# Quantised feed-forward: rows times their steps before the first product, and the last group of the feed-forward on VectorE alone

## The chip, the cores and the metric

The kernel runs on one core of a Trainium2 chip. Its engines are TensorE (PE; its weight loads are PEld), VectorE (DVE), ScalarE (ACT) and GpSimd (POOL); SyncE (SP) issues most transfers. Each engine works through its own instructions in order and waits for semaphores that the others raise. The metric is the device time of one execution in microseconds (us); lower is better.

## The reference, cut to what matters

The program is a cross-attention layer with a top-32 selection, a state-space convolution, a GELU feed-forward (phase "ff"), and a quantised feed-forward with a depthwise convolution (phase "bf"). The change touches the end of ff and all of bf. With T = 4096 rows, D = 512 and 2048 hidden features, bf computes:

```python
def act_quant(x):
    scale = 127.0 / jnp.clip(jnp.max(jnp.abs(x), axis=-1, keepdims=True), 1e-05)
    return jnp.clip(jnp.round(x * scale), -128, 127) / scale
def weight_quant(w):
    scale = 1.0 / jnp.clip(jnp.mean(jnp.abs(w)), 1e-05)
    return jnp.clip(jnp.round(w * scale), -1, 1) / scale
...
xq = x + jax.lax.stop_gradient(act_quant(x) - x)
wq = w + jax.lax.stop_gradient(weight_quant(w) - w)
...
h = bit_linear(x, w1)                               # rows quantised, weights -1, 0, 1
h = depthwise_conv1d(h.transpose(0, 2, 1), conv_w, conv_b)   # three taps along the rows
h = h.transpose(0, 2, 1)
h = jax.nn.silu(h)
return bit_linear(h, w2)                            # h quantised again by its row's maximum
...
x = x + _L0_xattn_ref(_layernorm(x, axis=-1), ...)
x = x + _L0_ffn_ref(_layernorm(x, axis=-1), ...)
```

So a row of the input of bf is a row of small integers (`q`, exact in bf16) times one number, its step.

## The kernel before, in words

**ff** (`feed_forward`) takes the 4096 rows in 8 groups (QUADS) of 4 tiles of 128 rows. The work that closes a group (add the second product, layer norm, add x, layer norm again, find each row's step, round, turn the integers on TensorE and store them) is laid between the products of the next group. Only the last group (`last_g`) has nothing beside it: its closing work stands after the last matmul. `out_moments`, `normalise_out`, `x_moments`, `normalise_x`, `find_steps`, `round_x` and `quantise_x` run on VectorE, each over all four tiles; between `normalise_out` and `x_moments` GpSimd (`back`) multiplies each tile by `g_norm_out` and adds it to `x`. TensorE turns the four tiles of `q` one after the other through one PSUM bank (`turn_q`), ScalarE copies each out (`copy_q`) and then stores all four at once into `scratch_qT`, at column 512 g + 1. Then all engines meet (`end_phase`), and bf begins.

**bf** (`bit_feed_forward`) takes the rows in 9 blocks of 456 (448 in the last). Step i = 8 n + j of 72 handles block n and the pair j of 8 pairs of 128 hidden features. In a step

- TensorE (`first`) makes 8 bf16 matmuls of 458 columns, integer weights times integer rows, into `hp[i % 2]`; it may do so once the taps of step i - 2 have read that bank;
- VectorE (`dequantise`) multiplies both halves in PSUM by `rowstep`, the steps of the rows spread over all partitions;
- ScalarE (`first_tap`) writes the first tap into `conv`, VectorE (`add_taps`) adds the other two with four instructions, ScalarE takes `silu`, then `measure` writes the absolute values into `size`, and VectorE (`raise_high`) keeps the maximum over the features in `high`.

After the eighth pair VectorE folds `high` to `top`, TensorE turns it (`turn_top`, step 8 n + 10), VectorE finds the rows' steps (`steps`, step 8 n + 11, after its taps), TensorE spreads them (`spread_steps`, step 8 n + 12) and ScalarE copies them (`copy_scale`, end of step 8 n + 12). That releases GpSimd for the block: 8 multiplications (`scaling`) and 3 roundings (`quantise`). ScalarE rounds the other five pairs (`round_up`, `round_down`) in steps 8 n + 14 to 8 n + 18. From step 8 n + 19 TensorE makes the second product (`second`: 8 bf16 matmuls of 512 columns in a step), and VectorE (`finish`) adds it to `x2`, four times in a block. The last block has its last five pairs scaled and rounded on VectorE (`quantise_last`).

SP loads the integers and steps of a block two ahead into double buffers, and loads and stores `x2` a block at a time. The order is written out by hand: the loops over i of each engine fix it.

Of the kernel before, what the change touches and what calls it, by code (L numbers as in the profile page):

```python
# [1818 lines left out]
def feed_forward(nc, sem, const, a, mean, dram):  # L1819
# [7 lines left out]
    with scope:  # L1827
# [43 lines left out]
            "xt_free", "qT_stored", "rowstep_stored", "x_stored", "biased", "edges", "passed")}  # L1871
# [5 lines left out]
        with nc.Block() as block:  # L1877
# [111 lines left out]
            def _(pool):  # L1989
# [48 lines left out]
            def _(dve):  # L2038
# [188 lines left out]
                round_x(last_g)  # L2227
                quantise_x(last_g)

            @block.scalar  # L2230
            def _(act):
# [4 lines left out]
                act.dma_start(dram["qT"][:, :, 0], zero[:], allow_slow_non_contiguous=True).then_inc(s["qT_stored"], 16)  # L2236
                act.dma_start(dram["qT"][:, :, T + 1], zero[:], allow_slow_non_contiguous=True).then_inc(s["qT_stored"], 16)
# [15 lines left out]
                def copy_q(g, k):  # L2253
# [3 lines left out]
                    nc.scalar.activation(qT[:, :, k * P:(k + 1) * P], fl[1][:].bitcast(BF16)[:, 0:D].rearrange("p (c t) -> p c t", t=P),  # L2257
# [62 lines left out]
                act.wait_ge(s["qT_stored"], 16 * (QUADS + 2))  # L2320
# [3 lines left out]
            def _(pe):  # L2324
# [116 lines left out]
def bit_feed_forward(nc, sem, const, a, mean, dram, out):  # L2441
# [9 lines left out]
    BY_ACT, LAST_BY_ACT = 5, 3  # L2451
    STEPS_AT, SCALE_AT, ROUND_AT, SECOND_AT = JC + 3, JC + 4, JC + 6, 2 * JC + 3
    with scope:
        W1q = sb("bf_W1q", [P, DC, HID], BF16)
        W2q = sb("bf_W2q", [P, FC, D], BF16)
        rowstep = sb("bf_rowstep", [P, 2, STEP + 2])
# [3 lines left out]
        qin = sb("bf_qin", [P, 2, DC, STEP + 2], BF16)  # L2460
        x2 = sb("bf_x2", [P, 2, QUAD, D])
# [33 lines left out]
        with nc.Block() as block:  # L2495
            @block.sync
            def _(sp):
                def load(n):

                    if n >= 2:  # L2500
                        sp.wait_ge(s["first_done"], JC * (n - 1))
                    sp.dma_start(qin[:, n % 2, :, 0:QUAD * rows(n) + 2],
                                 dram["qT"][:, :, STEP * n:STEP * n + QUAD * rows(n) + 2]).then_inc(s[f"q_in{n % 2}"], 16)

                def load_steps(n):

                    if n >= 2:
# [428 lines left out]
```

## Time and profile before

| | |
|---|---|
| median of 3 runs | 4088.72 us (4087.74 to 4088.88) |
| the profiled execution | 4093.82 us, its span 4092.0 us |
| end of the last ff matmul | 3557.3 us of the span |
| first and last bf matmul start | 3608.5 and about 4085.8 us |
| busy over the span | PE 77%, DVE 74%, ACT 55%, POOL 38% |

How to read it: times are microseconds from the start of the span; a row of a timeline has start, duration, engine, line, operation, out<-in, shapes, count, and in brackets how long the engine sat idle before and what released it. A row of windows has the stretch, its length, busy time and instruction count of each engine, the granted TensorE clock as a share of full speed (1.00 is 2.4 GHz, 0.50 is 1.2 GHz), the DMA share and the rate. bf16 and f32 are the types that the rows name; TensorE's operands that are declared as F32R are written f32 too.

### The profile page before, as it was taken

The numbers are of one execution on the slowest core, as the hardware profiler recorded it, in microseconds if no ns is written. First come the engines' busy times: TensorE is split into PE (matmuls) and PEld (weight loads), VectorE is DVE, ScalarE is ACT, GpSimd is POOL, SyncE is SP. The second block draws the span as 40 slices with busy tenths as digits, with TensorE's granted clock in tenths as the row PEclk, the third lists the DMA queues.
The fourth block names the chain that finished last, engine by engine and source line by source line (L and its number), as shares of the span: only waits on it lengthen the run. The fifth ranks groups of instructions, "written<-read, shape, count | busy, mean of one in ns | idle before, by whom it ended". The sixth has DMA issues, their size and how long they took to land. (4 is left out here: it accounts for less than half of the span.)

```text
span 4092.0 us, 53285 instructions
## 1 busy us (share of the span) xinstructions
PE 3136.8 (77%) x16624; PEld 1983.5 (48%) x16624; DVE 3013.2 (74%) x7501; ACT 2241.5 (55%) x2905; POOL 1561.5 (38%) x1275
## 2 busy tenths in 40 slices
PE   7545857878786688777978777599999999746776
PEld 3222424444443344445755554377777777612333
DVE  7699999999999999975579986234444444469996
ACT  4575959898986898861133332133333333247774
POOL 0024636665564556656201000213333322206664
PEclk9756878888877787888989988799999999868887
DMA  8700000000000000003214334544344443331111
GB/s 320 267 7 8 10 7 12 10 10 12 9 10 9 10 9 10 9 6 106 81 38 97 90 88 98 152 124 128 118 127 127 129 127 103 95 86 36 54 44 55
DMA packets 264316, 290.46 MB, mean 71 GB/s; under 512 B 55452, under 2 KB 177438, under 8 KB 263012
## 3 DMA queue, kind: packets, MB, share of 16 engines
q1 hardware_dynamic: 240728, 254.05, 20.7%
q10 hardware_dynamic: 20268, 18.34, 1.6%
q0 software_dynamic: 3040, 14.94, 0.9%
q8 instruction: 102, 1.67, 0.2%
q14 instruction: 178, 1.46, 0.1%
HBM read 218.82 MB, written 68.45 MB: 70 GB/s over the span
## 5 line engine op out<-in xcount | busy, mean ns | idle before, releaser
L1094 PE MATMUL up<-ctx,attnT 128*128 128x384 f32 (+1 forms) x1664 | 713.7, 585 | 41.6 <-ACT attnT L966 41.6
L1066 PE MATMUL score<-KT,q 64*128 64x512 f32 (+1 forms) x1792 | 388.4, 527 | 377.5 <-ACT S L928 279.6
L823 DVE MAX8 cand<-S 128x8 f32<-128x146 f32 (+1 forms) x2816 | 601.2, 296 | 57.6 <-ACT S L928 38.6
L782 POOL TENSOR_TENSOR S<-S 128x512 f32<-128x512 f32 (+1 forms) x224 | 424.6, 1928 | 351.5 <-DVE S L828 351.5
L1094 PEld LDWEIGHTS up<-ctx,attnT 128*128 128x128 f32 (+1 forms) x1664 | 365.6, 230 | 314.4 <-issue 154.8
L828 DVE SCALAR_TENSOR_TENSOR S<-S,tops,E 128x3202 f32<-128x3202 f32 x128 | 472.8, 3757 | 14.6 <-ACT E L957 14.6
L1066 PEld LDWEIGHTS score<-KT,q 64*128 64x128 f32 x1792 | 175.5, 239 | 580.1 <-ACT S L928 435.2
L928 ACT ACTIVATE S<-score 128x1024 f32<-128x1024 f32 (+1 forms) x448 | 402.8, 931 | 89.4 <-PE score L1066 88.8
L2163 DVE TENSOR_TENSOR ff_gelu<-ff_whole,ff_gelu 128x512 fp32r<-128x512 f32 x128 | 99.4, 777 | 429.7 <-ACT ff_gelu L2290 429.7
L935 ACT ACTIVATE E<-S,below 128x3202 bf16<-128x3202 f32 x128 | 379.6, 2966 | 38.6 <-DVE below L865 17.7
L957 ACT ACTIVATE E<-S,ebias 128x3202 f32<-128x3202 f32 x128 | 376.2, 2964 | 22.5 <-DVE S L828 12.4
L2399 PE MATMUL ff_acc<-ff_W,ff_gelu 128*128 128x512 f32 x1024 | 345.5, 398 | 0.0
L2289 ACT ACTIVATE ff_whole<-ff_fp,ff_b 128x512 f32<-128x512 f32 x128 | 87.8, 686 | 397.0 <-PE ff_fp L2384 396.7
L2384 PE MATMUL ff_fp<-ff_hT,ff_W 128*128 128x512 f32 x1024 | 267.2, 404 | 4.7 <-ACT ff_gelu L2290 3.2
L2761 PE MATMUL bf_hp<-bf_qin,bf_W1q 128*128 128x458 bf16 (+1 forms) x576 | 160.8, 435 | 117.7 <-DVE bf_conv L2602 98.1
L789 POOL TENSOR_TENSOR S<-S 128x512 f32<-128x512 f32 (+1 forms) x217 | 243.5, 1159 | 8.4 <-issue 8.4
L2556 POOL TENSOR_TENSOR bf_silu<-bf_silu,bf_scale 128x912 f32<-128x912 f32 (+1 forms) x67 | 162.6, 2465 | 212.9 <-ACT bf_scale L2713 212.9
L2399 PEld LDWEIGHTS ff_acc<-ff_W,ff_gelu 128*128 128x128 f32 x1024 | 193.5, 189 | 45.4
L2384 PEld LDWEIGHTS ff_fp<-ff_hT,ff_W 128*128 128x128 f32 x1024 | 190.9, 191 | 48.2 <-ACT ff_gelu L2290 4.1
L793 POOL TENSOR_TENSOR S<-S 128x512 f32<-128x512 f32 (+1 forms) x217 | 207.6, 992 | 4.9 <-issue 4.9
L2602 DVE SCALAR_TENSOR_TENSOR bf_conv<-bf_hp,bf_taps,bf_conv 128x456 f32<-128x456 f32 (+1 forms) x288 | 185.8, 687 | 25.2 <-ACT bf_conv L2686 14.3
L2399 PE MATMUL ff_acc<-ff_w_low,ff_gelu 128*128 128x512 f32 x512 | 203.1, 397 | 0.0
(378 smaller groups left out, 5890.7 us busy)
## 6 DMA issues: line engine op xcount, KB each, us to landing
s_hankel<-scratch_K SPq DMA_DIRECT2D x128, 256.0 KB, 4.4
ff_w_low<-scratch_w1l SPq DMA_DIRECT2D x112, 256.0 KB, 2.6
ff_w_low<-scratch_w2l SPq DMA_DIRECT2D x112, 256.0 KB, 2.7
xt_prep<-in_x SPq DMA_DIRECT2D x8, 1024.0 KB, 8.3
scratch_xt<-xt_prep SPq DMA_DIRECT2D x8, 1024.0 KB, 8.2
next_prep<-in_ffn_w_t POOLq DMA_DIRECT2D x8, 1024.0 KB, 11.3
q<-scratch_qt SPq DMA_DIRECT2D x128, 64.0 KB, 1.9
mod_xt<-in_x_turned SPq DMA_DIRECT2D x32, 256.0 KB, 2.7
```

The source lines that it names most:

```text
L782: nc.gpsimd.tensor_tensor(S[:, b, 0, chunk(j)], S[:, b, 0, chunk(j)], S[:, b, 1, chunk(j)], ALU.add).then_inc(s["summed01"], 1)
L789: nc.gpsimd.tensor_tensor(S[:, b, 0, chunk(j)], S[:, b, 0, chunk(j)], S[:, b, 2, chunk(j)], ALU.add).then_inc(s["summed02"], 1)
L793: nc.gpsimd.tensor_tensor(S[:, b, 0, chunk(j)], S[:, b, 0, chunk(j)], S[:, b, 3, chunk(j)], ALU.add).then_inc(s["summed"], 1)
L823: nc.vector.max(cand[:, h, 8 * k:8 * k + 8], S[:, b, h, k * SEG:min((k + 1) * SEG, G)])
L828: nc.vector.scalar_tensor_tensor(S[:, b, h, :], S[:, b, h, :], tops[:, b, h, TOP - 1:TOP], E[:, h % 2, :], ALU.is_ge, ALU.mult).then_inc(s ...
L928: nc.scalar.activation(S[:, b, PAIRS_OF_HEADS[p], chunk(j)], score[bank(p, j)][:, :, 0:w], ACT.Copy).then_inc(s["score_copied"], 1)
L935: nc.scalar.activation(signs, S[:, b, h, :], ACT.Sign, bias=below[:, h:h + 1], accum_out=count[:, h:h + 1]).then_inc(s["counted"], 1)
L957: nc.scalar.activation(E[:, h % 2, :], S[:, b, h, :], ACT.Exp, bias=ebias[:, b, h:h + 1], scale=SCALE).then_inc(s["e_ready"], 1)
L1066: last = nc.tensor.matmul(score[bank(p, j)][:, e, 0:w], lhsT=q[at, b, part, h // 2, :], rhs=KT[at, h // 2, chunk(j)], start=(part == 0), s ...
L1094: last = nc.tensor.matmul(up[:, 0:DV], lhsT=attnT[0:w, e, c - 4 * g, :], rhs=ctx[0:w, c, :], start=(c == 0), stop=(c == GC - 1))
L2384: last = nc.tensor.matmul(fp[f % 2][:], lhsT=left, rhs=hT[:, h_part, c, :], start=(j == 0), stop=(j == len(terms) - 1))
L2399: last = nc.tensor.matmul(acc[:, k, :], lhsT=gelu[:, g_part, F % RING, k * P:(k + 1) * P], rhs=right, start=(f == 0 and j == 0), stop=(f = ...
```

## The change: what it does

1. **Last group of ff.** GpSimd only adds `b_norm_out` to x (`x_shifted`) and takes no further part. VectorE does the multiplication by `g_norm_out` and the addition too, in an order that rotates through the tiles: in one round it normalises tile i, multiplies tile i - 1, adds tile i - 2 and takes the moments of tile i - 3, with a drain after each round. Rounding and quantising go tile by tile, the turned tiles use two PSUM banks in turn, and `qT` is stored in two halves of 256 columns.
2. **`scratch_qT`** has a margin of 32 columns at either end, so that a group's store starts at a multiple of 64 bytes.
3. **First product of bf.** A row's integers are multiplied by its step before the product: GpSimd (`spread`, for block 0 VectorE) writes `rows_of_x`, 4 x 458 columns, in f32; ScalarE (`high_x`) rounds it to F32R, VectorE (`low`) takes the rest, and TensorE multiplies both parts by the weights, now F32R as well: 16 matmuls in a step, where there were 8. `dequantise` goes. The weights come in as bf16 (into the second half of `bf_silu`, free at that time) and are cast by VectorE (pieces 0 and 1) and GpSimd (2 and 3).
4. **Order on ScalarE:** `first_tap(i)` now precedes `silu(i-1)`; it waits for TensorE and no longer for VectorE. The absolute values go back into `conv`.
5. **SP** loads one block of integers and steps at a time (single buffers), and loads and stores `x2` tile by tile.

```diff
-                add_hidden(last_g)
-                out_moments(last_g)
-                normalise_out(last_g)
-                x_moments(last_g)
...
+                for i in range(QUAD + 3):
+                    if i < QUAD:
+                        v.tensor_scalar(at[i], at[i], mv["out"][:, i, 0:1], rstd["out"][:, i:i + 1], ALU.subtract, ALU.mult)
+                    if 1 <= i < QUAD + 1:
+                        v.tensor_tensor(at[i - 1], at[i - 1], rows["g_norm_out"][:], ALU.mult)
+                    if 2 <= i < QUAD + 2:
+                        v.tensor_tensor(x[:, i - 2], x[:, i - 2], at[i - 2], ALU.add).then_inc(s["x_ready"], 1)
+                    if 3 <= i:
+                        v.bn_stats(stats["x"][:, i - 3, :], x[:, i - 3])
+                    dve.drain()
...
-                        act.dma_start(dram["qT"][:, :, QUAD * P * g + 1:QUAD * P * (g + 1) + 1], qT[:]).then_inc(s["qT_stored"], 16)
+                        act.dma_start(dram["qT"][:, :, MARGIN + QUAD * P * g:MARGIN + QUAD * P * (g + 1)], qT[:]).then_inc(s["qT_stored"], 16)
...
+    HIGH_AT, LOW_AT = 3, 4
...
-        W1q = sb("bf_W1q", [P, DC, HID], BF16)
+        W1q = sb("bf_W1q", [P, DC, HID], F32R)
...
+                def spread(n):
+                    w = QUAD * rows(n) + 2
+                    pool.wait_ge(s["q_in"], 32 * (n + 1))
+                    pool.wait_ge(s["parts_ready"], n)
+                    nc.gpsimd.tensor_tensor(rows_of_x[:, :, 0:w], qin[:, :, 0:w], rowstep[:, 0:w].unsqueeze(1).broadcast_to([P, DC, w]),
+                                            ALU.mult).then_inc(s["dequantised"], 1)
...
                 for n in range(BLOCKS - 1):
+                    if n + 2 < BLOCKS:
+                        spread(n + 2)
                     pool.wait_ge(s["scale_ready"], n + 1)
...
-                    for e in range(2):
-                        at = hp[i % 2][:, e, 0:w]
-                        v.tensor_tensor(at, at, rowstep[:, n % 2, 0:w], ALU.mult).then_inc(s["dequantised"], 1)
+                    dve.wait_ge(s["high_ready"], n + 1)
+                    v.tensor_tensor(x_parts[:, n % 2, 1, :, 0:w], rows_of_x[:, :, 0:w], x_parts[:, n % 2, 0, :, 0:w].bitcast(F32),
+                                    ALU.subtract).then_inc(s["parts_ready"], 1)
...
+                def high_x(n):
+                    w = QUAD * rows(n) + 2
+                    act.wait_ge(s["dequantised"], n + 1)
+                    if n >= 2:
+                        act.wait_ge(s["first_done"], JC * (n - 1))
+                    nc.scalar.activation(x_parts[:, n % 2, 0, :, 0:w], rows_of_x[:, :, 0:w], ACT.Copy).then_inc(s["high_ready"], 1)
...
                 for i in range(ALL + ROUND_AT):
+                    if i % JC == HIGH_AT and i < ALL - JC:
+                        high_x(i // JC + 1)
...
+                    for x in range(2):
+                        if j == 0 and x == 1:
+                            pe.wait_ge(s["parts_ready"], n + 1)
+                        for e in range(2):
+                            f = 2 * j + e
+                            for c in range(DC):
+                                last = nc.tensor.matmul(hp[i % 2][:, e, 0:w], lhsT=W1q[:, c, f * P:(f + 1) * P], rhs=x_parts[:, n % 2, x, c, 0:w],
+                                                        start=(c == 0 and x == 0), stop=(c == DC - 1 and x == 1))
```

VectorE's order at the end of ff, before: each operation over the four tiles, with GpSimd's part between the second and third of these rows.

```order
L2102 TENSOR_SCALAR ff_xt<-ff_xt,ff_mv_out,ff_rstd_out 128x512 x4
L2108 BN_STATS ff_stats_x<-ff_x 128x6 x4
L2058 BN_AGGR ff_mv_x<-ff_stats_x 128x2 x4
L2063 RECIPROCAL ff_rstd_x<-ff_rstd_x 128x4
L2114 TENSOR_SCALAR ff_xt<-ff_x,ff_mv_x,ff_rstd_x 128x512 x4
```

And now, in the same place:

```order
L2240 TENSOR_SCALAR ff_xt<-ff_xt,ff_mv_out,ff_rstd_out 128x512 x2
L2242 TENSOR_TENSOR ff_xt<-ff_xt,ff_g_norm_out 128x512
L2240 TENSOR_SCALAR ff_xt<-ff_xt,ff_mv_out,ff_rstd_out 128x512
L2242 TENSOR_TENSOR ff_xt<-ff_xt,ff_g_norm_out 128x512
L2244 TENSOR_TENSOR ff_x<-ff_x,ff_xt 128x512
L2240 TENSOR_SCALAR ff_xt<-ff_xt,ff_mv_out,ff_rstd_out 128x512
L2242 TENSOR_TENSOR ff_xt<-ff_xt,ff_g_norm_out 128x512
L2244 TENSOR_TENSOR ff_x<-ff_x,ff_xt 128x512
L2246 BN_STATS ff_stats_x<-ff_x 128x6
```

GpSimd's multiplication and addition have moved between the normalisations, to VectorE.

GpSimd in bf, before, from its first block on (`bf_silu` is the block's values, `bf_gq` the rounded ones):

```order
L2556 TENSOR_TENSOR bf_silu<-bf_silu,bf_scale 128x912 x8
L2564 TENSOR_SCALAR bf_gq<-bf_silu 128x912 x3
L2556 TENSOR_TENSOR bf_silu<-bf_silu,bf_scale 128x912 x8
L2564 TENSOR_SCALAR bf_gq<-bf_silu 128x912 x3
L2556 TENSOR_TENSOR bf_silu<-bf_silu,bf_scale 128x912 x8
```

And now (`bf_rows` is `rows_of_x`):

```order
L2601 TENSOR_TENSOR bf_rows<-bf_qin,bf_rowstep 128x1832
L2620 CAST bf_W1q<-bf_silu 128x4x512 x2
L2601 TENSOR_TENSOR bf_rows<-bf_qin,bf_rowstep 128x1832
L2606 TENSOR_TENSOR bf_silu<-bf_silu,bf_scale 128x912 x8
L2614 TENSOR_SCALAR bf_gq<-bf_silu 128x912 x3
L2601 TENSOR_TENSOR bf_rows<-bf_qin,bf_rowstep 128x1832
L2606 TENSOR_TENSOR bf_silu<-bf_silu,bf_scale 128x912 x8
L2614 TENSOR_SCALAR bf_gq<-bf_silu 128x912 x3
```

One multiplication of 1832 columns stands behind the three roundings of each block.

ScalarE in bf, steps 8 n + 3 and 8 n + 4, before:

```order
L2698 ACTIVATE bf_silu<-bf_conv 128x912
L2686 ACTIVATE bf_conv<-bf_hp,bf_tap_bias,bf_taps 128x456 x2
L2706 ACTIVATE bf_size<-bf_silu 128x912
L2698 ACTIVATE bf_silu<-bf_conv 128x912
L2686 ACTIVATE bf_conv<-bf_hp,bf_tap_bias,bf_taps 128x456 x2
L2706 ACTIVATE bf_size<-bf_silu 128x912
L2713 ACTIVATE bf_scale<-bf_step_rows 128x456
```

And now:

```order
L2742 ACTIVATE bf_x_parts<-bf_rows 128x1832
L2753 ACTIVATE bf_conv<-bf_hp,bf_tap_bias,bf_taps 128x456 x2
L2765 ACTIVATE bf_silu<-bf_conv 128x912
L2771 ACTIVATE bf_conv<-bf_silu 128x912
L2753 ACTIVATE bf_conv<-bf_hp,bf_tap_bias,bf_taps 128x456 x2
L2765 ACTIVATE bf_silu<-bf_conv 128x912
L2771 ACTIVATE bf_conv<-bf_silu 128x912
L2778 ACTIVATE bf_scale<-bf_step_rows 128x456
```

The copy of the next block's rows (`high_x`) stands ahead of the first tap of step 8 n + 3; the first tap has moved ahead of the silu.

## Rows read from the trace of the kernel before

**Rows 1.** Windows: four blocks of bf by their first dequantise, and a stretch of ff.
```profile
3611.90:3652.40 40.50, 22.35 (x64) 7.51 (x62) 35.02 (x54) 24.03 (x31) 0.00 (x0) 0.63 0.38 142
3652.40:3697.10 44.70, 25.23 (x70) 8.91 (x70) 41.09 (x67) 28.79 (x37) 18.01 (x8) 0.66 0.06 16
3697.10:3744.20 47.10, 28.73 (x118) 13.78 (x118) 43.14 (x68) 34.67 (x43) 31.93 (x13) 0.92 0.06 16
...
3888.40:3936.50 48.10, 34.61 (x134) 17.13 (x134) 44.49 (x70) 34.89 (x43) 28.99 (x12) 0.85 0.16 54
...
3400.00:3550.00 150.00, 148.14 (x664) 118.16 (x663) 58.50 (x108) 47.74 (x73) 29.63 (x20) 1.00 0.38 108
```

**Rows 2.** Waits from 3500 us on: who waited for whom, total, times, longest.
```profile
PE bf_hp L2761 <- DVE bf_conv L2602: 98.1, 47, 4.5
```

**Rows 3.** Timeline of VectorE in the sixth block of bf.
```profile
3862.48 0.68 DVE L2625 TENSOR_REDUCE bf_most<-bf_mp 114x4 f32<-114x512 f32 x1
...
3864.86 1.18 DVE L2590 TENSOR_TENSOR bf_hp<-bf_hp,bf_rowstep 128x458 f32<-128x458 f32 x2
...
3877.41 1.11 DVE L2616 TENSOR_TENSOR bf_high<-bf_size,bf_high 128x912 f32<-128x912 f32 x1
3878.62 2.66 DVE L2602 SCALAR_TENSOR_TENSOR bf_conv<-bf_hp,bf_taps,bf_conv 128x456 f32<-128x456 f32 x4
3881.20 0.74 DVE L2644 SCALAR_TENSOR_TENSOR bf_x<-bf_op,bf_undo,bf_x 114x512 f32<-114x512 f32 x1
...
3883.12 2.51 DVE L2616 TENSOR_TENSOR bf_high<-bf_size,bf_high 128x912 f32<-128x912 f32 x1
```

**Rows 4.** Timeline of GpSimd: the eighth block's scaling and rounding.
```profile
4012.31 19.22 POOL L2556 TENSOR_TENSOR bf_silu<-bf_silu,bf_scale 128x912 f32<-128x912 f32 x8 [18.84 <-ACT bf_scale L2713]
4031.48 9.74 POOL L2564 TENSOR_SCALAR bf_gq<-bf_silu 128x912 bf16<-128x912 f32 x3
```

**Rows 5.** Timeline of ScalarE: a first tap, and the copy that releases Rows 4.
```profile
3889.29 1.34 ACT L2686 ACTIVATE bf_conv<-bf_hp,bf_tap_bias,bf_taps 128x456 f32<-128x456 f32 x2
...
4011.68 0.54 ACT L2713 ACTIVATE bf_scale<-bf_step_rows 128x456 f32<-128x456 f32 x1
```

**Rows 6.** Groups by form, ScalarE and GpSimd: count, then busy us, mean ns.
```profile
L541 ACT ACTIVATE junk_prep<-next_prep 128x2048 bf16<-128x2048 f32 x8 | 15.3, 1911 | 0.7
...
L2017 POOL TENSOR_TENSOR ff_x<-ff_x,ff_b_norm_out 128x2048 f32<-128x2048 f32 x8 | 36.9, 4615 | 58.3 <-DMA ff_x<-in_x 58.3
...
L2556 POOL TENSOR_TENSOR bf_silu<-bf_silu,bf_scale 128x896 f32<-128x896 f32 x3 | 8.3, 2785 | 6.6 <-ACT bf_scale L2713 6.6
```

**Rows 7.** Timeline of TensorE: F32R in ff, then bf's start and sixth block.
```profile
3527.96 2.03 PE L2384 MATMUL ff_fp<-ff_hT,ff_W 128*128 128x512 f32 x8
...
3608.54 6.01 PE L2761 MATMUL bf_hp<-bf_qin,bf_W1q 128*128 128x458 bf16 x16 [19.47 <-DMA bf_W1q<-scratch_w1q]
...
3865.00 1.03 PE L2779 MATMUL bf_step_rows<-bf_diag,bf_every 114*128 114x456 f32 x2 [1.45 <-DVE bf_diag L2635]
...
3881.42 1.72 PE L2761 MATMUL bf_hp<-bf_qin,bf_W1q 128*128 128x458 bf16 x8
3882.98 1.89 PE L2797 MATMUL bf_op<-bf_W2q,bf_gq 128*114 128x512 bf16 x8
```

**Rows 8.** Timeline of VectorE and ScalarE at the end of ff.
```profile
3563.46 3.81 DVE L2102 TENSOR_SCALAR ff_xt<-ff_xt,ff_mv_out,ff_rstd_out 128x512 f32<-128x512 f32 x4
...
3576.84 1.92 DVE L2114 TENSOR_SCALAR ff_xt<-ff_x,ff_mv_x,ff_rstd_x 128x512 f32<-128x512 f32 x4
...
3583.84 1.43 DVE L2140 TENSOR_SCALAR ff_q<-ff_xt 128x512 bf16<-128x512 f32 x4
...
3589.11 0.60 ACT L2257 ACTIVATE ff_qT<-ff_fl 128x512 bf16<-128x512 bf16 x1 [0.76 <-PE ff_fl L2367]
```

**Rows 9.** DMA issues from 3580 us to 3625 us: size, us to landing.
```profile
scratch_qT<-ff_qT ACTq DMA_DIRECT2D x1, 512.0 KB, 11.0
```

**Rows 10.** Windows: the last store.
```profile
4088.00:4090.00 2.00, 0.00 (x0) 0.00 (x0) 0.00 (x0) 0.00 (x0) 0.00 (x0) 0.65 1.00 310
```

More of the change, by code:

```diff
@@ L1812 @@
 LEAST = 1e-5
+MARGIN = 32
 LEVEL = 127.0
@@ new lines, in load_x, with store @@
+                def load_x(n, k):
+                    if n >= 1:
+                        sp.wait_ge(s[f"stored{k}"], 16 * n)
+                    sp.dma_start(x2[0:rows(n), k], dram["x2"][rows_at(n, k), :]).then_inc(s[f"x_in{k}"], 16)
+                def store(n, k):
+                    sp.wait_ge(s["y_ready"], QUAD * n + k + 1)
+                    sp.dma_start(out[rows_at(n, k), :], x2[0:rows(n), k]).then_inc(s[f"stored{k}"], 16)
+                load(0)
+                for k in range(HID // BANK):
+                    sp.dma_start(raw_w1[:, :, k * BANK:(k + 1) * BANK], dram["w1q"][:, :, k * BANK:(k + 1) * BANK]).then_inc(s[f"w1_in{k}"], 16)
+                    if k == 0:
+                        sp.dma_start(taps[:], a["conv_w_cols"]).then_inc(s["taps_in"], 16)
+                        sp.dma_start(tap_bias[:], a["conv_b_cols"]).then_inc(s["taps_in"], 16)
@@ L2545, in _ @@
-                for b in range(2):
-                    sp.wait_ge(s[f"stored{b}"], 16 * ((BLOCKS + 1 - b) // 2))
+                for k in range(QUAD):
+                    load_x(0, k)
+                for m in range(BLOCKS + 3):
+                    if m + 2 < BLOCKS:
+                        load(m + 2)
+                    if 0 <= m - 3 < BLOCKS:
+                        store(m - 3, 2)
+                    if 0 <= m - 3 < BLOCKS - 1:
+                        load_x(m - 2, 1)
+                    if 0 <= m - 3 < BLOCKS:
+                        store(m - 3, 3)
+                    if 0 <= m - 3 < BLOCKS - 1:
+                        load_x(m - 2, 2)
+                    if 0 <= m - 2 < BLOCKS:
+                        store(m - 2, 0)
+                    if 0 <= m - 3 < BLOCKS - 1:
+                        load_x(m - 2, 3)
+                    if 0 <= m - 2 < BLOCKS:
+                        store(m - 2, 1)
+                    if 0 <= m - 2 < BLOCKS - 1:
+                        load_x(m - 1, 0)
@@ L2548, in _ @@
+                for k in range(QUAD):
+                    sp.wait_ge(s[f"stored{k}"], 16 * BLOCKS)
             @block.gpsimd
@@ L2668, in _ @@
                         steps((i - STEPS_AT) // JC)
+                    if i % JC == LOW_AT and i < ALL - JC:
+                        low(i // JC + 1)
                     if i == ALL - JC + SCALE_AT:
@@ L2703, in measure @@
                     act.wait_ge(s["silu_done"], i + 1)
[L2704 to L2706 removed]
+                    nc.scalar.activation(conv[:, j % DEEP, :, 0:QUAD * rows(n)], part(n, j), ACT.Abs).then_inc(s["sized"], 1)
                 def copy_scale(n):
```

166 lines of the change are left out of this document (83 added, 83 removed).

## The prediction, made before the changed kernel was run

> **What bounds the kernel now.** I read the stretches first, then the waits, then the timelines of single engines. The change reaches the end of ff and all of bf, 535 us of 4092; the rest I leave as it is. In bf a block takes 40.5 us at the start and 48.1 us from the fourth on, and VectorE is busy for 44.5 of these 48.1, TensorE for 34.6 and GpSimd for 29.0 [rows 1]. TensorE waits for the taps on VectorE, 98.1 us in 47 waits [rows 2]. So VectorE sets the pace. One step costs it: dequantise 1.27 us (3864.86 to the next instruction, 1.18 busy and a drain), the maximum 1.21 (3877.41 to 3878.62), the four tap instructions 2.58 (3878.62 to 3881.20), together 5.06 [rows 3], and 8 x 5.06 = 40.5 is the first block exactly. The rest of a later block is the steps (2.38, 3862.48 to 3864.86), four finishes of 0.74, one fold, and stretched maxima such as the one of 2.51 us instead of 1.11 [rows 3].
>
> **The change in bf, part by part.**
> VectorE loses 16 dequantise instructions a block, 8 x 1.27 = 10.2 us, and gains one `low` of 1832 columns: two SBUF inputs in f32, by the maximum's 1.11 us for 912 columns at most 2.2, I take 2.1 [rows 3]. Its busy time in a block falls from 44.5 to about 36 us, and it is no longer the bound.
>
> TensorE's first product doubles to 16 matmuls of 458 columns, now F32R. The trace has F32R only at 512 columns: 8 in 2.03 us with the last one's 0.4, a pitch of 0.233 [rows 7]. The bf16 matmul of 458 columns has 1.56 / 8 = 0.195 (3881.42 to 3882.98) and that of 512 (1.89 - 0.38) / 7 = 0.216 [rows 7]. So F32R has 0.017 more at 512. If that is a constant, 458 columns take 0.21, which I use; the bounds are 0.195 (no surcharge) and 0.233 (the weight load sets the pitch, whatever the columns). A block costs TensorE 8 x (16 x 0.21 + 8 x 0.216) = 40.7, the spread of the steps 0.9, four small transposes 0.6 at most by the 458-column pitch: 42.1 us, with bounds of 40.1 and 45.
>
> The Trainium skill (TensorE: Matmul & The Clock Gate, Weight-path perf modes) says that the fast weight load works for 128 weights of any type but FP32. It speaks against the change, since the weights become F32R; by it the pitch would be nearer the upper bound, and that is the first rival below.
>
> GpSimd gains `spread`, 1832 columns with two inputs. By the 2048-column addition of 4.615 us (2.25 ns a column) it costs 4.1, by the scaling at 19.22 / 8 = 2.40 for 912 columns (2.63 ns) 4.8; at the rounding's 9.74 / 3 = 3.25 (3.6 ns) it would be 6.5 [rows 4, 6]. I take 4.7. It stands behind the block's roundings, and ScalarE's `high_x` of the next but one block waits for it ahead of the first tap of step 8 n + 3, in front of everything that leads to the next `copy_scale`. That closes a loop: scaling and rounding 28.9 [rows 4], spread 4.7, high_x 1.73 (the 2048-column activation takes 1.91, less 216 columns) [rows 6], first tap 1.34 [rows 5], taps 2.66 and steps 2.38 [rows 3], spread_steps 1.03 [rows 7], copy_scale 0.54 [rows 5]: 43.3 us. Seven handovers of 0.08 (ScalarE ends at 4012.22, GpSimd starts at 4012.31) [rows 4, 5] make it 43.9. Queued behind the waiting high_x are the taps, so VectorE, and two steps later TensorE, wait with it. The loop is 1.8 longer than TensorE's own 42.1 and is what I expect to be late next. ScalarE itself carries 34.9 [rows 1] + 1.7, about 37 of 43.9.
>
> Blocks, before and after: the first is 8 x 3.79 (maximum and taps) + 2.1 - 1.2 (no maximum for its first pair) plus some start-up, 33.0 against 40.5, -7.5. The second has steps, fold and low beside: 36.5 against 44.7, -8.2. The third gets the second product and the loop: 44.5 against 47.1, -2.6. Blocks four to eight: 5 x (43.9 - 48.1) = -21. The steps of the ninth up to `copy_scale` of the eighth: no high_x, -2. From there on (4012.2 to the end) the chain is as before: GpSimd scales and rounds 28.9, then second product, `quantise_last`, second product; 0.
>
> The start of bf is later. Before, the first matmul starts at 3608.5 when the weights are in, at half the clock: 16 matmuls in 6.01, 0.376 each [rows 7]. Now VectorE first multiplies (2.1), ScalarE copies (1.73) while VectorE casts the weights, with two handovers 4.0; then step 0 has 16 matmuls at half clock instead of 8, +3.0; the first dequantise before the tap goes, -0.7. Together +6.3. The rows' steps, whose load now gates the start, I take as landing with the weights. GpSimd's two casts are hidden: pairs 4 and 6 are wanted 16 and 24 us after the first.
>
> Sum in bf up to the last store: 6.3 - 7.5 - 8.2 - 2.6 - 21 - 2 = -35.0.
>
> **The end of ff.** From 3563.46 to 3576.84 the chain takes 13.4 us: normalisation at 3.81 for four, since GpSimd works beside it, where the next one takes 1.92 without [rows 8], then GpSimd's product and sum tile by tile. On VectorE alone it is 1.9 + 12 x 0.62 (512 of 912 columns at 1.11) [rows 3] + seven drains of 0.15 + the same 1.1 of aggregate and root = 11.5, -1.9; the drains of the rotated first part give back 0.6. Rounding tile by tile lets the first transpose start 1.2 earlier; the last copy, now at 3589.71 because each turn and copy through one bank takes 1.36, follows VectorE's pitch of 0.95: -1.3 [rows 8]. Together -3.8.
>
> The store of `qT` lands 11.0 us after its issue [rows 9], and no engine computes in that time. It goes to 2-byte aligned columns; now the last half of 256 KB starts on a 64-byte multiple. Bounds: 11 (alignment does nothing) and 3; I take 4.5, so -6.5.
>
> The last store: 896 KB at 310 GB/s take 2.9 us [rows 10]; now only the last quarter is left: -2.0.
>
> Sum: -35.0 - 3.8 - 6.5 - 2.0 = -47.3. Against the profiled execution's 4093.8 that is 4046.5; that execution is 5.1 us above the median of the runs, so the median should be 4041, and I say 4042.
>
> **Rivals.**
> A. TensorE is the bound: F32R at 458 columns keeps the pitch of 0.233. Block 45 us plus one handover, 45.3; against 43.9 that is 1.4 x 5 and about 3 in the earlier blocks: +10, 4052. For: 0.233 is measured, 0.21 is not. Against: nothing in the rows says that the pitch is the load's and not the columns'.
> B. GpSimd is slower than taken: the scaling takes 2.785 when VectorE uses SBUF all the time [rows 6] against 2.40 [rows 4], 8 x 0.38 = 3.1 a block, or `spread` takes 6.5. Loop 45.7 to 47, six blocks: +11 to +18, 4056. For: VectorE's maxima are stretched beside GpSimd now, 2.51 for 1.11 [rows 3]. Against: VectorE has fewer instructions than before. The Trainium skill (GPSIMD Engine Reference, Specifications) says that GpSimd shares its SBUF interfaces with VectorE and that they contend when VectorE has two SBUF inputs; `low` and the maxima are such. The trace agrees for the maxima, and by that rule this rival gains.
> C. The store of `qT` is no faster: +6.5, 4049.
> D. Slower than before: TensorE falls back to 1.2 GHz. Its mean clock in bf is 0.63 to 0.92 of full now [rows 1], and at half clock a step costs 16 x 0.376 + 8 x 0.42 (0.376 by the columns) = 9.4, a block 78. With 30% of the matmuls there a block is 42.1 + 0.3 x 36 = 53: (53 - 43.9) x 8 = +73, 4115. It turns the sign from a share of about 22% on. Against: in ff, where TensorE is busy for 148 of 150 us, the clock is 1.00 [rows 1], and here it would be busy for 42 of 44.
>
> The change certainly does what it says; the instructions are counted in the order.
>
> **Chances.** Forecast (4036 to 4048) 0.50, A 0.17, B 0.15, C 0.10, D 0.05, the rest (a faster GpSimd or a gain in the early blocks) 0.03. The range of 8 in 10 takes in the bounds of the pitch, the store and `spread`: 4029 to 4062. About 0.2% (8 us) is what a measurement of this kernel tells from no change: faster 0.94, same 0.02, slower 0.04.
>
> **What would show it.** A steady block of 43.9 us between first taps; ScalarE waiting for `bf_rows` at high_x once a block, about 1 to 2 us; TensorE's clock at 1.00 from the third block on; F32R pitch of 0.21 in `bf_hp`; GpSimd's new instruction at 4.7 us; first taps of bf some 6 us later after the weights; `qT` landing under 5 us. If TensorE has no wait left in a steady block, A holds; if high_x waits long and the block is over 45, B; a clock under 0.8 in steady blocks would make the whole forecast wrong.

## The result, and the profile after

The changed kernel takes 4064.73 us (4064.64 to 4065.74, 4 runs) against 4088.80 us before (4087.74 to 4089.04): a ratio of 0.9942, 95% interval 0.9925 to 0.9959. A second measurement gave 4063.50 us against 4090.17 (0.9934, 0.9918 to 0.9951). So it is faster, by 24 us and not by the 47 forecast; 4064.7 lies outside the range of 4029 to 4062.

The work ahead of the changed part ends at 3557.3 us in the trace of before and at 3553.3 after, though it is the same; in twelve more traces it ends between 3549.0 and 3557.9. So I count from marks: the end of the last ff matmul, the start of bf (GpSimd's first memset), GpSimd's first scaling of each block. The stretch from the start of bf to the first scaling is 71.5 to 73.9 us in the eleven other traces of the changed bf and its variants, so a difference of 2 us in that row says little.

| us | before | after | change | forecast |
|---|---|---|---|---|
| last ff matmul to start of bf | 44.8 | 39.9 | -4.9 | -10.3 |
| start of bf to 1st scaling | 77.0 | 71.9 | -5.1 | -5.3 |
| 1st to 2nd | 45.0 | 47.2 | +2.2 | -5.4 |
| 2nd to 8th | 288.2 | 270.7 | -17.5 | -24.3 |
| 8th to the end | 79.7 | 79.8 | +0.1 | -2.0 |
| sum | | | -25.2 | -47.3 |

The forecast's column is made of its own terms: +6.3 - 7.5 and half of -8.2 up to the first scaling (it comes at the end of step 12), the other half of -8.2 and of -2.6 to the second, and the rest behind.

Windows of the changed kernel, which answer to [rows 1] (stretch, length, busy time and count of PE, PEld, DVE, ACT, POOL, clock, DMA share, GB/s). First the first block by its taps, then the stretch from first to second scaling, then a steady block.

```profile
3610.09:3644.91 34.82, 27.91 (x127) 23.09 (x126) 29.38 (x39) 26.70 (x33) 9.41 (x4) 1.00 0.28 83
3665.16:3712.37 47.21, 37.31 (x152) 29.71 (x151) 41.63 (x50) 36.21 (x44) 36.11 (x12) 0.90 0.05 16
3848.49:3893.89 45.40, 42.76 (x199) 32.91 (x199) 40.87 (x55) 36.77 (x44) 35.51 (x12) 1.00 0.19 58
```

VectorE's 44.5 of 48.1 have become 40.9 of 45.4, TensorE's 34.6 have become 42.8 at a clock of 1.00. No engine is busy all the time. The waits from 3740 to 3990 us (who for whom, total, times, longest) show who holds whom:

```profile
ACT bf_conv L2753 <- PE bf_hp L2833: 30.9, 14, 4.4
...
PE bf_step_rows L2851 <- DVE bf_diag L2689: 8.2, 5, 2.0
...
ACT bf_x_parts L2742 <- POOL bf_rows L2601: 3.2, 4, 0.9
...
PE bf_hp L2833 <- DVE bf_conv L2654: 2.9, 5, 1.0
```

TensorE's 98.1 us of waiting for the taps [rows 2] have become 17.0 over the same part of the program, and 2.9 in this window. What is left is mainly a wait for the steps once a block, and ScalarE's wait for GpSimd's `rows_of_x`. GpSimd's timeline of one block, to set beside [rows 4]:

```profile
3848.49 21.42 POOL L2606 TENSOR_TENSOR bf_silu<-bf_silu,bf_scale 128x912 f32<-128x912 f32 x8 [9.90 <-ACT bf_scale L2778]
3869.88 10.56 POOL L2614 TENSOR_SCALAR bf_gq<-bf_silu 128x912 bf16<-128x912 f32 x3
3880.41 3.59 POOL L2601 TENSOR_TENSOR bf_rows<-bf_qin,bf_rowstep 128x1832 f32<-128x1832 bf16 x1
3893.89 21.34 POOL L2606 TENSOR_TENSOR bf_silu<-bf_silu,bf_scale 128x912 f32<-128x912 f32 x8 [9.89 <-ACT bf_scale L2778]
```

21.4 + 10.55 + 3.6 + 9.9 = 45.4: that is the whole block. ScalarE and TensorE between `spread` and the next scale, in the same block:

```profile
3884.03 1.73 ACT L2742 ACTIVATE bf_x_parts<-bf_rows 128x1832 fp32r<-128x1832 f32 x1 [0.94 <-POOL bf_rows L2601]
3885.67 1.34 ACT L2753 ACTIVATE bf_conv<-bf_hp,bf_tap_bias,bf_taps 128x456 f32<-128x456 f32 x2
...
3893.27 0.55 ACT L2778 ACTIVATE bf_scale<-bf_step_rows 128x456 f32<-128x456 f32 x1 [1.32 <-PE bf_step_rows L2851]
```

```profile
3863.61 3.58 PE L2833 MATMUL bf_hp<-bf_x_parts,bf_W1q 128*128 128x458 f32 x16
3867.03 1.89 PE L2869 MATMUL bf_op<-bf_W2q,bf_gq 128*114 128x512 bf16 x8
...
3892.20 1.03 PE L2851 MATMUL bf_step_rows<-bf_diag,bf_every 114*128 114x456 f32 x2 [2.04 <-DVE bf_diag L2689]
```

`high_x` starts as soon as GpSimd is done, and everything up to `bf_scale` follows it: so the loop of the prediction is closed. Sixteen F32R matmuls take 3867.03 - 3863.61 = 3.42 us, 0.214 each (forecast 0.21, against 0.376 at half clock in [rows 7]).

### The profile page after: what moved, and what is told of

Read it like the earlier page. It is cut to its first block and busy times, and to the rows that moved or that the text cites. A ratio compares the mean times of both kernels' runs of the same rounds, so it can differ in the third digit from the quotient of the medians.

```text
span 4062.9 us, 54357 instructions
## 1 busy us (share of the span) xinstructions
PE 3210.7 (79%) x17200; PEld 2131.9 (52%) x17200; DVE 2987.0 (74%) x7377; ACT 2258.4 (56%) x2914; POOL 1602.9 (39%) x1277
## 5 line engine op out<-in xcount | busy, mean ns | idle before, releaser
L1094 PE MATMUL up<-ctx,attnT 128*128 128x384 f32 (+1 forms) x1664 | 710.9, 582 | 40.9 <-ACT attnT L966 40.9
L2833 PE MATMUL bf_hp<-bf_x_parts,bf_W1q 128*128 128x458 f32 (+1 forms) x1152 | 271.2, 389 | 39.3 <-ACT bf_x_parts L2742 22.4
L2833 PEld LDWEIGHTS bf_hp<-bf_x_parts,bf_W1q 128*128 128x128 f32 x1152 | 222.2, 195 | 78.0 <-issue 32.6
L2606 POOL TENSOR_TENSOR bf_silu<-bf_silu,bf_scale 128x912 f32<-128x912 f32 (+1 forms) x67 | 178.3, 2700 | 110.7 <-ACT bf_scale L2778 110.7
## 6 DMA issues: line engine op xcount, KB each, us to landing
next_prep<-in_ffn_w_t POOLq DMA_DIRECT2D x8, 1024.0 KB, 11.3
```

The lines of the kernel that those rows point to most:

```text
L1094: last = nc.tensor.matmul(up[:, 0:DV], lhsT=attnT[0:w, e, c - 4 * g, :], rhs=ctx[0:w, c, :], start=(c == 0), stop=(c == GC - 1))
L2606: nc.gpsimd.tensor_tensor(part(n, j), part(n, j), scale[:, n % 2, 0:QUAD * rows(n)].unsqueeze(1).broadcast_to([P, 2, QUAD * rows(n)]), ALU ...
L2833: last = nc.tensor.matmul(hp[i % 2][:, e, 0:w], lhsT=W1q[:, c, f * P:(f + 1) * P], rhs=x_parts[:, n % 2, x, c, 0:w], start=(c == 0 and x = ...
```

## The experiments

Each was timed beside the kernel before on the same chip. The kernel before had medians of 4088.3, 4091.5 and 4090.2 us in the three groups of four, so ratios are to be compared, and for single stretches the traces.

**1. The end of ff alone.** bf is that of before, reading qT at the new offset.

```diff
                     sp.dma_start(qin[:, n % 2, :, 0:QUAD * rows(n) + 2],
-                                 dram["qT"][:, :, STEP * n:STEP * n + QUAD * rows(n) + 2]).then_inc(s[f"q_in{n % 2}"], 16)
+                                 dram["qT"][:, :, MARGIN - 1 + STEP * n:MARGIN - 1 + STEP * n + QUAD * rows(n) + 2]).then_inc(s[f"q_in{n % 2}"], 16)
```

> The kernel before with the changed end of ff alone (last group on VectorE, aligned halves of qT); bf as before. By the trace of the changed kernel the closing work is 4.1 us shorter and the time from the last copy to bf 0.7 us shorter: 4084 us. If the end of ff were worth what was predicted for it (3.8 and 6.5 us) it would be 4078.5 us. If it were nothing by itself, 4089 us.

4085.61 us against 4088.27, ratio 0.9994 (0.9985 to 1.0003): the time alone can't tell 0 from 6 us. The stretch from the last ff matmul to bf is 38.2 us in its trace; nine traces of kernels that share this code have 38.2 to 39.9, before has 44.8. So the part is worth 4.9 to 6.6 us by the traces, not 10.3. In the changed kernel 4.1 of its 4.9 are the closing work, so the store itself brought 0.8.

**2. The last group's steps stored early, by SP.**

```diff
-                    if k == 0:
+                    if k == 0 and g < QUADS - 1:
                         act.wait_ge(s["rowstep_stored"], 16 * (g + 2))
...
+                sp.wait_ge(s["rowstep_made"], QUADS)
...
+                sp.dma_start(dram["rowstep"][QUAD * P * last + 1:QUAD * P * QUADS + 1].rearrange("(k p) -> p k", p=P), rowstep[:, last % 2], ...)
```

> The changed kernel, but the last group's row steps (2 KB in 512 packets of 4 bytes) are stored by SP as soon as they are made, some 4 us earlier and on a queue of their own. Theory: those packets, not qT's alignment, fill the 8 us before bf; they took until 12.7 us after their issue, so bf starts 5 us sooner and the time is 4060 us; qT itself lands 3 to 5 us after its issue. Rival: the landing of qT's own 512-byte runs takes 10.7 us whatever else is stored: 4065 us and 10.7 us again.

Ratio 0.9938 (0.9925 to 0.9952), 4061.51 us. The store of the steps starts at 3571.99 of its trace, 2.1 us before the first copy of qT and not 4; the stretch is 36.3 us, where the nine traces have 38.2 to 39.9, and qT's halves land in 7.0. The direction is the theory's, the size 1.9 to 3.6 us of the 5 expected; the runs lie between 4056.8 and 4067.1, so the time by itself shows nothing here. What made me look there are these windows of the changed kernel behind the issues of qT's halves at 3579.82 and 3581.62:

```profile
3581.00:3582.00 1.00, 0.00 (x0) 0.00 (x0) 0.00 (x0) 0.59 (x1) 0.00 (x0) 0.50 2.03 250
3584.00:3585.00 1.00, 0.00 (x0) 0.00 (x0) 0.00 (x0) 0.00 (x0) 0.00 (x0) 0.50 1.10 4
3588.00:3589.00 1.00, 0.00 (x0) 0.00 (x0) 0.00 (x0) 0.00 (x0) 0.00 (x0) 0.50 0.70 9
```

In the first of these microseconds the DMA engines move 250 GB/s; in the two later ones the share is 1.10 and 0.70 and they move 4 and 9 GB/s (the share adds up the time of all packets and can pass 1). Busy at next to no bytes made me suspect tiny packets: the steps are 512 elements of 4 bytes, each in a place of its own.

**3. The steps turned, then stored in four runs.**

```diff
+                nc.tensor.transpose(fl[1][0:QUAD, 0:P], rowstep[:, (QUADS - 1) % 2], const["ident"][:]).then_inc(s["rowstep_turned"], 1)
...
+                nc.scalar.activation(last_steps[:], fl[1][0:QUAD, 0:P], ACT.Copy).then_inc(s["rowstep_copied"], 1)
...
+                act.dma_start(dram["rowstep"][QUAD * P * (QUADS - 1) + 1:QUAD * P * QUADS + 1].rearrange("(k p) -> k p", p=P), last_steps[:]).then_inc(s["rowstep_stored"], 16)
```

> The changed kernel, but TensorE turns the last group's row steps and they are stored as 4 runs of 512 bytes instead of 512 packets of 4. Theory: only the 4-byte packets were slow, so qT's halves land some 3 us after their issue and bf starts 7 us sooner than in the changed kernel: 4057.5 us. Rival: 512-byte runs of qT are slow by themselves (7 us to landing when the steps went by another queue): as there, 4061 us.

Ratio 0.9922 (0.9905 to 0.9938), 4059.12 us. The stretch falls to 32.3 us, 6.5 less than in the traces of experiments 6 and 10, timed beside it (38.8 each). The issue rows (size, us to landing), first of the changed kernel, answering to [rows 9], then of this one:

```profile
scratch_qT<-ff_qT ACTq DMA_DIRECT2D x2, 256.0 KB, 10.7
```

```profile
scratch_qT<-ff_qT ACTq DMA_DIRECT2D x2, 256.0 KB, 2.7
```

The same halves of qT, in the same runs of bytes and to the same place, land in 2.7 us where no 4-byte packets go ahead of them. The rows of ScalarE's DMA queue from 3577 to 3594 us (packets, MB, the time that they took as a share of 16 engines), again first the changed kernel, show the packets themselves:

```profile
q10 hardware_dynamic: 1584, 0.53, 63.8%
```

```profile
q10 hardware_dynamic: 1064, 0.53, 10.6%
```

520 packets fewer at the same bytes take the share from 63.8% to 10.6%. The steps are also issued earlier here, 2.9 us ahead of qT's first half instead of 1.4; but in experiment 2 it was 3.6 us, with the 4-byte packets, and the halves still took 7.0. So it is the packets and not the time of issue. Experiment 12 has the same store, and again 2.7 and 32.3 us. The Trainium skill (DMA: Bandwidth & Descriptors, Specifications) says that transfers under 512 bytes are done by read-modify-write. The traces show the price, 6.5 us on the path, and not the mechanism.

**4. The alignment alone.**

```diff
-MARGIN = 32
+MARGIN = 1
```

> The changed kernel with a margin of 1 column: qT's halves start at 2-byte multiples, as before the change, all else the same. By the theory that the 4-byte packets set the landing: 10.7 us and 4065 us again. By the prediction's (alignment is worth 6.5 us or some of it): a landing of over 12 us and 4067 to 4071 us.

Ratio 0.9946 (0.993 to 0.9963), 4069.73 us. The landing is 12.2 us, against 9.0 to 10.7 in the nine traces with the aligned store, and the stretch 42.0, 2.1 to 3.8 longer than in them. So my theory, that the packets are all of it, failed, and the numbers given above for the other side came true (over 12 us, 4067 to 4071). By this one trace alignment is worth 2 to 4 us with the 4-byte packets ahead; the prediction's 6.5 was too much. Without those packets it was not measured.

**5. `spread` out of the loop on GpSimd.**

```diff
-                    if n + 2 < BLOCKS:
-                        spread(n + 2)
+                    if n == 0:
+                        spread(2)
...
                     for j in range(JC):
                         scaling(n, j)
+                        if j == BY_ACT - 1 and n + 3 < BLOCKS:
+                            spread(n + 3)
```

> The changed kernel, but GpSimd makes the rows of a block (spread) after the fifth scaling of the block before instead of behind its roundings. Theory: the loop scaling 21.4, rounding 10.6, spread 3.6, copy to scale 9.9 = 45.4 us sets the block; with spread out of it ScalarE's high_x waits for nothing, TensorE's 42.9 busy plus a handover is next, a block takes 43.4, the stretch between the first two scalings also loses 3: about -14, 4051 us. Rival: TensorE or VectorE sets the block already and GpSimd only ends with it: 45.4 a block and 4065 us.

Ratio 0.9942 (0.9929 to 0.9956), 4064.41 us: no change, and the theory's number failed. The stretch to the second scaling does fall, 47.2 to 45.2, but the first scaling comes 1.9 us later in this trace (beside a clock of 0.72 from 3635.8 to 3641.8, where the changed kernel has 1.00), the steady block stays 45.4, and that although `high_x` waits for nothing. Its TensorE:

```profile
3870.45 3.63 PE L2835 MATMUL bf_hp<-bf_x_parts,bf_W1q 128*128 128x458 f32 x16 [1.10 <-DVE bf_conv L2656]
...
3884.60 1.94 PE L2871 MATMUL bf_op<-bf_W2q,bf_gq 128*114 128x512 bf16 x8
...
3892.60 1.03 PE L2853 MATMUL bf_step_rows<-bf_diag,bf_every 114*128 114x456 f32 x2 [0.99 <-DVE bf_diag L2691]
```

and the row of VectorE ahead of that first wait, with a maximum that took 3.00 us where it takes 1.11 undisturbed:

```profile
3864.65 3.00 DVE L2672 TENSOR_TENSOR bf_high<-bf_conv,bf_high 128x912 f32<-128x912 f32 x1
```

TensorE now waits for VectorE's taps and steps, 1.10, 0.50 and 0.99 in this block; with its 42.8 of work that is the block. The text of the next experiment named a second loop instead (roundings, second product, next scale). Its rows don't bear it out: the roundings end at 3884.39, TensorE's product starts at 3884.60 with no wait shown before it. Whether that loop would have held it at the same length can't be told from this.

**6. `high_x` and `low` moved behind the scale.**

```diff
-    HIGH_AT, LOW_AT = 3, 4
+    HIGH_AT, LOW_AT = 5, 5
```

> The changed kernel, but ScalarE's high_x and VectorE's low stand in step 8 n + 5, behind copy_scale, instead of steps 8 n + 3 and 8 n + 4. Theory: moving spread on GpSimd brought nothing since a second loop of the same length took over (the roundings end, the second product's first step, the steps' spreading in the step behind it, the scale, the scalings); with high_x moved, GpSimd's own order stays, the first loop is cut and the second has 42 us, so TensorE's 42.9 busy is next: a block of 43.4, about -12, 4052 us. Rival: the block is set by something both have in common (45.4 in both kernels): 45.4 again and 4065 us.

Ratio 0.9948 (0.9932 to 0.9965), 4071.16 us; most blocks take 46.8, longer than before. The wait for the steps is gone (0.2 us in all), a new one has come, VectorE and then TensorE:

```profile
3859.36 3.36 DVE L2641 TENSOR_TENSOR bf_x_parts<-bf_rows,bf_x_parts 128x1832 fp32r<-128x1832 f32 x1
3862.81 2.89 DVE L2670 TENSOR_TENSOR bf_high<-bf_conv,bf_high 128x912 f32<-128x912 f32 x1
```

```profile
3868.60 3.58 PE L2833 MATMUL bf_hp<-bf_x_parts,bf_W1q 128*128 128x458 f32 x16 [2.81 <-DVE bf_conv L2654]
```

`low` and the maximum behind it take 6.3 us, where undisturbed they take 2.06 and 1.11, in the middle of GpSimd's scalings. So what the traces of 5 and 6 have in common is time lost between these two engines.

**7. Without `low`.** From the third block on the remainder of the rows is left out.

```diff
-                    w = QUAD * rows(n) + 2
+                    w = QUAD * rows(n) + 2 if n < 2 else 8
```

> The changed kernel without low (the remainder of the rows) from the third block on: VectorE writes 8 columns instead of 1832, TensorE multiplies what stood there. Theory: GpSimd stands still while low's two inputs are read: the eight scalings of a block fall from 21.4 to 19.3 us, the loop from 45.4 to 43.3, 7 blocks: 4050 us. Rival: the scalings are slowed by the denser maxima and taps: they stay at 21.4 and the time at 4064 us.

Ratio 0.9908 (0.9893 to 0.9923), 4052.66 us. GpSimd:

```profile
3844.28 19.56 POOL L2606 TENSOR_TENSOR bf_silu<-bf_silu,bf_scale 128x912 f32<-128x912 f32 x8 [9.90 <-ACT bf_scale L2778]
3863.80 10.57 POOL L2614 TENSOR_SCALAR bf_gq<-bf_silu 128x912 bf16<-128x912 f32 x3
3874.34 3.58 POOL L2601 TENSOR_TENSOR bf_rows<-bf_qin,bf_rowstep 128x1832 f32<-128x1832 bf16 x1
```

The eight scalings lose 1.9 of the 2.06 us that `low` takes: GpSimd had stood still for nearly all of it. The scalings one by one show it still better. First the changed kernel's second scaling of a block, beside which `low` runs, then the second and third here:

```profile
3850.63 4.06 POOL L2606 TENSOR_TENSOR bf_silu<-bf_silu,bf_scale 128x912 f32<-128x912 f32 x1
```

```profile
3846.41 2.16 POOL L2606 TENSOR_TENSOR bf_silu<-bf_silu,bf_scale 128x912 f32<-128x912 f32 x1
3848.53 3.04 POOL L2606 TENSOR_TENSOR bf_silu<-bf_silu,bf_scale 128x912 f32<-128x912 f32 x1
```

Five of the eight take 2.13 to 2.17 us. The three that begin while a maximum on VectorE is under way take 3.04 or 3.05, and the one that began with `low` took 4.06. The maximum that starts here at 3847.33, in the middle of the second scaling, takes 2.20 us instead of 1.11: it too waits until the other engine is done. The block is 19.56 + 10.57 + 3.58 + 9.90 = 43.6, as measured. The Trainium skill (SBUF — State Buffer, SBUF: two separate sides) says that a VectorE instruction with two SBUF inputs and a GpSimd instruction lock each other out for the whole instruction. The trace agrees, by 1.9 for `low`'s 2.06 and by 0.9 for a maximum's 1.11.

**8. `low` where GpSimd is idle.** LOW_AT is 3 and the call stands ahead of the taps.

```diff
+                    if i % JC == LOW_AT and i < ALL - JC:
+                        low(i // JC + 1)
                     if i < ALL:
                         add_taps(i)
...
-                    if i % JC == LOW_AT and i < ALL - JC:
-                        low(i // JC + 1)
```

> The changed kernel, but VectorE's low stands ahead of the taps of step 8 n + 3, right behind high_x, where VectorE waits 2.14 us for the first tap and GpSimd is idle until the next scale. Theory: low no longer stops the scalings (21.4 to 19.5 us, as without low) and costs the taps behind it 0.8: a block of 44.3, 4057 us. Rival: low's 2.06 us stand in the loop in full, between high_x and the taps, and undo what GpSimd gains: 45.6 and 4065 us.

Ratio 0.9924 (0.9908 to 0.9941), 4058.97 us, a block of 44.2 to 44.5: 19.53 + 10.56 + 3.60 + 10.74 = 44.4. Nothing is left out, and the scalings have the time that they have without `low`:

```profile
3846.81 19.53 POOL L2606 TENSOR_TENSOR bf_silu<-bf_silu,bf_scale 128x912 f32<-128x912 f32 x8 [10.74 <-ACT bf_scale L2778]
```

```profile
3882.23 2.07 DVE L2641 TENSOR_TENSOR bf_x_parts<-bf_rows,bf_x_parts 128x1832 fp32r<-128x1832 f32 x1 [0.83 <-ACT bf_x_parts L2742]
```

**9. Six pairs rounded by ScalarE.** BY_ACT is 6 and ROUND_AT one step earlier.

```diff
-    BY_ACT, LAST_BY_ACT = 5, 3
+    BY_ACT, LAST_BY_ACT = 6, 3
...
-    STEPS_AT, SCALE_AT, ROUND_AT, SECOND_AT = JC + 3, JC + 4, JC + 6, 2 * JC + 3
+    STEPS_AT, SCALE_AT, ROUND_AT, SECOND_AT = JC + 3, JC + 4, JC + 5, 2 * JC + 3
```

> The changed kernel, but ScalarE rounds six of the eight pairs instead of five, one step earlier, and GpSimd two. Theory: both loops through GpSimd (spread to high_x, and the roundings to the second product to the next scale) lose one rounding of 3.5 us and fall to 41.9; TensorE, with no wait left, has a floor of 43.4 to 44 a block (8 steps of 5.07, the small transposes and the steps' spreading): 7 periods lose 1.4 to 2 and the second, of 47.2, some 3: 4052 us. Rival: VectorE and GpSimd slow each other wherever the work is put, as when high_x was moved (46.8 a block with a low of 3.36 and a maximum of 2.89 us): 45 to 46 and 4062 to 4068 us.

Ratio 0.9911 (0.9895 to 0.9928), 4054.45 us; 44.3 to 44.4 a block, 44.6 to the second scaling. `high_x` waits for nothing; TensorE still waits 1.0 for the steps and 0.5 for taps once a block. That is just over the expected floor of 43.4 to 44.

**10. The last steps spread ahead of the eighth block's second product.**

```diff
+                    if i == ALL + STEPS_AT % JC:
+                        spread_steps(BLOCKS - 1)
                     if i >= SECOND_AT:
                         second(i - SECOND_AT)
...
-                    if i % JC == SCALE_AT % JC and SCALE_AT <= i < ALL + SCALE_AT:
+                    if i % JC == SCALE_AT % JC and SCALE_AT <= i < ALL:
```

> The changed kernel, but TensorE spreads the last block's steps before the second product of the eighth block, which waits for GpSimd's roundings. Theory: the last scale is ready at 4010.7 instead of 4021.3, VectorE's last scaling and rounding start 10.9 us sooner, and the last second product begins at 4025.9 instead of 4036.5: 4054 us. Rival: GpSimd, which is busy with the eighth block until 4013.9, or the wait of the second product for finish keeps the end where it is: 4062 to 4065 us.

Ratio 0.992 (0.9903 to 0.9937), 4059.21 us. From the eighth scaling to the end 71.5 us instead of 79.8, -8.3. First the changed kernel's TensorE, then this one's:

```profile
4014.03 6.46 PE L2869 MATMUL bf_op<-bf_W2q,bf_gq 128*114 128x512 bf16 x16 [7.57 <-issue]
4020.33 0.92 PE L2851 MATMUL bf_step_rows<-bf_diag,bf_every 112*128 112x448 f32 x2
```

```profile
4013.22 1.86 PE L2851 MATMUL bf_step_rows<-bf_diag,bf_every 112*128 112x448 f32 x2 [3.20 <-DVE bf_diag L2689]
4017.29 9.52 PE L2869 MATMUL bf_op<-bf_W2q,bf_gq 128*114 128x512 bf16 x32 [2.20 <-issue]
```

The last scale no longer waits for roundings that it does not need. Of the expected 10.9 us the last scaling on VectorE gains 9.4, counted from the eighth scaling on GpSimd: the steps' spreading takes 1.86 at the lower clock instead of 0.92. VectorE's own work gives back 0.3 (14.2 us from its first scaling to the first `finish`, 13.8 in the changed kernel), and the last product 0.7 (23.48 against 22.76).

**11. The changed kernel once more.**

> The changed kernel itself, once more, on the chip of the three runs beside it. All theories: ratio to the kernel before 0.994 (4064.7 against 4088.8). By the traces so far the stretch from ff's last matmul to bf varies from 38.2 to 39.9 us among kernels that share this part, the block not at all: 45.4 us again.

Ratio 0.9934; the stretch before bf 39.0, blocks of 45.3 us and one of 46.0. As expected but for that one, which says how far a single block can vary.

**12. All of it together:** 3, 8, 9 and 10.

> The changed kernel with all that the runs point to: the last steps turned and stored in four runs (-6.5 by the stretch between ff and bf), the last steps spread before the eighth block's second product (-8.3), six pairs rounded by ScalarE and low ahead of the taps (-12 together by TensorE's floor of 43.4 a block). If they add up: 4038 us, 0.9875 of the kernel before. Rival: TensorE's clock falls or VectorE's floor holds a block at 45: 4048 us.

4037.61 us (4036.22 to 4039.63) against 4090.17, ratio 0.9872 (0.9855 to 0.9888). The stretch before bf is 32.3, steady blocks are 43.7 (one of 45.2), and `high_x` waits for nothing. This version beats both kernels, and the parts add up: 4038 us was expected. One by one, against the 4064.7 of the changed kernel, they had given 5.6, 5.8, 10.3 and 5.5 us.

## Why the prediction was wrong

The measured gain is 22.1 us short of the forecast. By the table 5.4 of these lie between ff's last matmul and bf, 0.2 in the first block and its steps, 7.6 between the first and the second scaling, 6.8 from there to the eighth, and 2.1 at the end.

- **VectorE no longer the bound, TensorE's pitch:** right. 40.9 of 45.4; 0.214. Rival A (0.233) is out, and so is D: the clock is 1.00 in steady blocks. VectorE's busy time was forecast at 36, though: in each block several maxima take 1.5 to 2.3 us instead of the 1.11 that the sum has.
- **Start of bf:** up to the first scaling -5.1 for a forecast of -5.3. Its terms were each a little too large: first taps 16.9 us after SP's first issue instead of 12.1 before (+4.8, not +6.3, since the clock rose within the first step), the first eight steps 34.8 instead of 40.7 (-5.9, not -7.5). That the sum fits is luck: the two errors cancel.
- **The loop and its price:** the loop was the right mechanism, its terms for GpSimd were not. Scaling and rounding stood at 28.9, the time that they had before; they take 32.0. Of these 3.1 us 1.9 are `low` (experiment 7) and 0.8 are the first rounding, which takes 4.1 beside a maximum and 3.25 without. `spread` was put at 4.7 and takes 3.6. Together 45.4 for 43.9. From the second to the eighth scaling that makes +6.8: 1.5 to 1.7 in each of four periods and 2.0 in the last, less 1.5 in the first, for which the forecast's third block was too long. It is rival B's mechanism at 1.5 us a block, and a little under B's loop of 45.7. The prediction named `low` as one that contends with GpSimd, and put no price on it in the loop.
- **Second and third block:** this is the step that failed most, by 7.6 us. The prediction let the second block run at 36.5, with "steps, fold and low beside", and applied the loop from the third on; but `high_x` waits for GpSimd already between the first and second scaling (1.56 us, at 3701.30). Its own loop would have given 43.9 there, 4.3 more than the 39.6 of its terms. The other 3.3 are the 1.5 by which the loop was too short, 0.8 of a rounding (11.3 for three instead of 10.55), and some 0.9 of the steps' spreading, 1.89 us instead of 1.03, since TensorE's clock is down. TensorE stood idle for 3.3 and 3.0 us before the spreading of the first and second block's steps, and in the windows behind, the clock is at 1.2 GHz for part or all of the time; in the steady block it stood idle for 2.04 at that place and the clock stayed at 1.00.

```profile
3660.00:3670.00 10.00, 7.39 (x21) 5.87 (x22) 9.35 (x17) 3.42 (x6) 4.84 (x2) 0.66 0.00 0
3710.00:3715.00 5.00, 5.00 (x12) 3.70 (x13) 4.83 (x6) 0.55 (x1) 2.63 (x2) 0.50 0.02 3
```

- **End of ff:** right; the closing work is 4.1 us shorter (forecast 3.8).
- **Store of qT:** this step failed too: forecast -6.5 by alignment, measured 11.0 to 10.7 at landing, and 9.0 to 10.7 in the nine traces. The 4.5 us that it took for the landing came from no row. The step took the row's name for its cause. The 4-byte packets of the steps were in front of it (experiment 3), a row of 2 KB that the prediction never read. What rival C named, a store no faster, came nearly true; the prediction gave no reason for it.
- **The end:** the last store is 2.3 us shorter (forecast 2.0), but the eighth block's GpSimd work is 1.9 longer and TensorE's 16 matmuls behind it run at a lower clock, 6.46 us for 5.07; from the first of the last eight `finish` to the last it is 0.9 shorter. Together that is +0.1 for a forecast of -2.0, which had only the last store.

Open: whether experiment 5 was held by VectorE alone or also by the roundings ahead of the second product. And the time of experiment 1 does not by itself confirm what its trace shows. What alignment is worth once the 4-byte packets are gone was not measured either.

## What to carry to other kernels

When a loop through several engines is priced, each of its instructions is to be taken at its duration beside the new neighbours, not at that of the old trace: here a VectorE instruction with two SBUF inputs stopped GpSimd for nearly its whole length. Apply the loop from the first block in which it can close. And when a transfer lands late, read what the DMA engines move while they are busy: a high share at a few GB/s points at tiny packets queued ahead, however few bytes they hold.

## What the runs showed of the hardware

512 packets of 4 bytes (2 KB) kept the DMA engines busy for some 8 us and delayed the landing of two stores of 256 KB behind them on their queue from 2.7 us to between 9.0 and 10.7. One GpSimd scaling of 912 columns takes 2.1 us, 3.0 when it begins beside a VectorE maximum of 1.11 us with two SBUF inputs, and 4.06 beside a subtraction of 2.06 us with two SBUF inputs. In the other direction that maximum takes 1.5 to 3.2 us beside GpSimd in the changed kernel. An F32R matmul of 458 columns with 128x128 weights follows the one before it in 0.214 us at full clock, a bf16 one in 0.195 [rows 7].
